# A smooth-quantised block of one decoder kernel: rounding in one pass, maxima and scaling read from PSUM, small operations merged over the batches, and the first product made turned

## The reference, cut to what matters

```python
def _smooth_quant_linear(x, w):
    amax_x = jnp.max(jnp.abs(x), axis=0)
    amax_w = jnp.max(jnp.abs(w), axis=0)
    s = jnp.sqrt(jnp.maximum(amax_x, EPS) / jnp.maximum(amax_w, EPS))
    s = jnp.maximum(s, EPS)
    xs = x / s
    ws = w * s
    x_scale = jnp.maximum(jnp.max(jnp.abs(xs), axis=-1, keepdims=True), EPS) / QMAX
    w_scale = jnp.maximum(jnp.max(jnp.abs(ws), axis=-1, keepdims=True), EPS) / QMAX
    x_q = jnp.clip(jnp.round(xs / x_scale), -QMAX, QMAX)
    w_q = jnp.clip(jnp.round(ws / w_scale), -QMAX, QMAX)
    return x_q @ w_q.T * x_scale * w_scale.T

def _expert_forward(xe, guw, dw):
    h = _smooth_quant_linear(xe, guw)
    gate, up = jnp.split(h, 2, axis=-1)
    a = jax.nn.silu(gate) * up
    return _smooth_quant_linear(a, dw)
```

## Time and profile before

| | us |
|---|---|
| median of three runs (2284.93 to 2288.26) | 2285.59 |
| the profiled execution | 2295.51 |
| its span, from first to last instruction | 2292.0 |
| the stage in it, from 587.01 (VectorE's first norm) to the end of the last addition on GpSimd | 81.6 |

### The profile page before, as it was taken

The page is one execution under the profiler, slowest core; times in us unless marked ns, Lnnn a source line. Parts: engine busy times, 40 slices in busy tenths (PEclk is TensorE's granted clock), DMA queues, the critical chain, the costliest instruction groups (busy, mean ns, idle before and its releaser), DMA issues.

```text
span 2292.0 us, 25579 instructions
## 1 busy us (share of the span) xinstructions
PE 1893.9 (83%) x9043; PEld 1207.4 (53%) x9048; DVE 1282.8 (56%) x2985; ACT 770.6 (34%) x1813; POOL 268.1 (12%) x254
## 2 busy tenths in 40 slices
PE   5685666888459599999856949899999899998698
PEld 3441223645345366666544636455555477777455
DVE  5738998654864444444487476433333666665222
ACT  4115454104122133333430612333332455554111
POOL 2611000000113200000020020000000222220111
PEclk9796877989758799999976979999999899999799
DMA  3010000000433300000000030300000200001300
GB/s 144 1 44 11 0 0 20 14 15 2 188 132 111 113 0 1 1 1 0 27 11 1 2 148 1 129 1 1 1 0 1 112 1 1 1 1 47 127 28 18
DMA packets 17373, 83.39 MB, mean 36 GB/s; under 512 B 3137, under 2 KB 9925, under 8 KB 13153
## 3 DMA queue, kind: packets, MB, share of 16 engines
q1 hardware_dynamic: 11168, 71.61, 7.9%
q0 software_dynamic: 2944, 8.03, 1.2%
q10 hardware_dynamic: 3136, 2.13, 0.3%
HBM read 73.49 MB, written 8.81 MB: 36 GB/s over the span
## 4 chain that ended last, share of the span: by engine, by line
PE 69%; DVE 18%; issue 6%; POOL 3%; ACT 2%; DMA 1%; another core or an unknown queue 0%; POOLq 0%; SPq 0%; DVEq 0%; ACTq 0%
PE bank L136 56%; PE bank L141 8%; PE bank L3330 3%; DVE space L795 2%; PE bank L3352 2%; DVE space L784 2%; DVE space L2881 1%; DVE space L1359 1%; DVE space L178 1%; DMA space<-in_L_attn 1%; POOL space L625 1%; POOL space L639 1%; ACT space L2936 0%; DVE space L1521 0%; DVE space L272 0%
## 5 line engine op out<-in xcount | busy, mean ns | idle before, releaser
L136 PE MATMUL bank<-space 128*128 128x256 f32 (+15 forms) x6725 | 1460.7, 426 | 102.3 <-DVE space L2881 18.5
L136 PEld LDWEIGHTS bank<-space 128*128 128x128 f32 (+7 forms) x6730 | 893.0, 183 | 621.0 <-issue 394.5
L141 PE MATMUL bank<-consts,space 128*128 128x128 f32 (+1 forms) x1610 | 259.9, 306 | 213.7 <-DVE space L189 67.0
L141 PEld LDWEIGHTS bank<-consts,space 128*128 128x128 f32 (+1 forms) x1610 | 205.8, 155 | 283.1 <-issue 157.3
L136 PE MATMUL bank<-space,consts 128*128 128x512 f32 (+2 forms) x148 | 90.8, 751 | 56.2 <-DVE space L790 49.1
L197 POOL TENSOR_TENSOR space<-space,consts 128x4 f32<-128x4 f32 x22 | 24.9, 1131 | 637.8 <-DVE space L184 637.8
L2571 POOL TENSOR_TENSOR space<-space,consts 128x4 f32<-128x4 f32 x64 | 68.6, 1072 | 220.7 <-DVE space L2502 220.7
L2320 DVE TENSOR_REDUCE space<-bank 128x2 f32<-128x512 f32 x64 | 44.0, 688 | 86.9 <-PE bank L136 86.8
L2366 ACT ACTIVATE space<-bank,space 128x256 f32<-128x256 f32 x128 | 59.5, 470 | 95.7 <-DVE space L2320 95.7
L136 PEld LDWEIGHTS bank<-space,consts 128*128 128x128 f32 x148 | 31.8, 237 | 99.2 <-DVE space L790 70.5
L2494 DVE TENSOR_REDUCE space<-bank 128x2 f32<-128x512 f32 x64 | 44.2, 691 | 71.1 <-PE bank L136 71.1
(11 more groups left out here) (344 smaller groups left out, 1983.2 us busy)
## 6 DMA issues: line engine op xcount, KB each, us to landing
space<-in_L_ffn SPq DMA_DIRECT2D x13, 2048.0 KB, 12.3
space<-in_L_attn SPq DMA_DIRECT2D x10, 2048.0 KB, 13.3
space<-in_L_xattn SPq DMA_DIRECT2D x4, 2048.0 KB, 9.7
expert_results<-space SPq DMA_DIRECT2D x16, 128.0 KB, 2.9
space<-expert_results SPq DMA_DIRECT2D x8, 256.0 KB, 4.7
space<-in_L_xattn SPq DMA_DIRECT2D x1, 1919.0 KB, 20.1
space<-in_L_xattn SPq DMA_DIRECT2D x1, 1536.0 KB, 6.2
space<-in_L_attn SPq DMA_DIRECT2D x1, 1074.5 KB, 4.9
```

What stands on the lines that cost most here:

```text
L136: return self.nc.tensor.matmul(out, lhsT, rhs, start=first, stop=last, skip_group_check=True)
L141: return self.nc.tensor.transpose(out, src, eye)
```

## The change

Both classes are rewritten; nothing else is touched. What is done after it:

- All small operations cover the four batches at once (`aw`, `ax`, `factor`, `inverse`, `scale`, `unit` are one tile each for all batches). The matrix maxima of `up` are taken first, those of `down` already during `up` (`weigh`).
- The maxima of the normed tokens are read from the PSUM banks into which they were turned, and ScalarE scales them from there into SBUF (`scale_tokens`); the copies of `Turned` are gone. VectorE scales `up`'s matrix; in `down` VectorE scales the tokens and ScalarE the matrix.
- TensorE turns the tokens (banks 4 to 7) and directly after them the matrix (banks 0 to 3), and VectorE takes the row maxima of both before anything is rounded.
- Rounding is one pass: times the reciprocal scale plus ROUND, left in f32. ScalarE does it for all tokens and for matrix batches 1 and 3 (Identity with a scale and a bias, both a column of SBUF), VectorE for matrix batches 0 and 2. The clips are gone. TensorE turns the f32 values (before: bf16), and the subtraction of ROUND is done by the copy from PSUM to bf16.
- The row of scales is a product of the scale column, broadcast to 128x128 as weights, with the identity, two of 128 columns per batch (before: one of 256 columns). The diagonal is gone.
- The first product is made turned (`tokens_out=False`): outputs on partitions, tokens along the row. Its tail is one multiplication with the row of token scales (`timed`), silu with the matrix scale, one `scalar_tensor_tensor` (`gated`) and the maximum for `down`; the eight turns and four copies between the linears are gone.
- At the end VectorE adds to x; GpSimd has only the norm's two operations left.

The removed lines are those of the functions above, marked "..." here.

```diff
 class SmoothLinear:
     N = 2
...
+    def __init__(self, c, w, kc, xs, rounded, tokens_out):
+        self.c, self.w, self.kc, self.xs, self.tokens_out = c, w, kc, xs, tokens_out
...
+        self.scale, self.unit = [c.sb(B, self.N) for _ in range(2)], [c.sb(B, self.N) for _ in range(2)]
+        self.t, self.row = rounded, c.bufs(B, S)
+        self.q = [[c.sb(kc, S, dt=BF16) for _ in range(B)] for _ in range(2)]
         self.s = c.signals(
...
     def tensor(self, e):
...
+        c, s, bk, n, kc, width = self.c, self.s, self.c.banks, self.N, self.kc, self.width
+        for b in range(B):
+            e.wait_ge(*s.x_scaled(b + 1))
+            self.back(bk[4 + b], self.xs(b)).then_inc(*s.x_back.one)
+        for b in range(B):
+            e.wait_ge(*s.w_scaled(b + 1))
+            self.back(bk[b], self.w(b)).then_inc(*s.w_back.one)
+        for b in range(B):
+            e.wait_ge(*s.x_rounded(b + 1))
+            self.again(bk[4 + b], self.t[0][b]).then_inc(*s.x_turned.one)
+        for b in range(B):
+            e.wait_ge(*(s.w_by_scalar if b % 2 else s.w_by_vector)(b // 2 + 1))
+            self.again(bk[b], self.t[1][b]).then_inc(*s.w_turned.one)
+        for b in range(B):
+            e.wait_ge(*(s.x_by_scalar if b % 2 else s.x_by_vector)(b // 2 + 1))
+            if self.tokens_out:
+                e.wait_ge(*(s.wq_by_scalar if b % 2 else s.wq_by_vector)(b // 2 + 1))
+            row = bk[b if self.tokens_out else 4 + b]
+            for i in range(n):
+                done = c.mm(row[:, i * P:(i + 1) * P],
+                            self.scale[1 if self.tokens_out else 0][:, b, i:i + 1].broadcast_to([P, P]), c.ident)
+            done.then_inc(*s.row_mm.one)
+            if not self.tokens_out:
+                e.wait_ge(*(s.wq_by_scalar if b % 2 else s.wq_by_vector)(b // 2 + 1))
+            left, right, out = (self.q[0][b], self.q[1][b], bk[4 + b]) if self.tokens_out else (self.q[1][b], self.q[0][b], bk[b])
+            for i in range(n):
                 for k in range(kc):
...
+                    done = c.mm(out[:, i * S:(i + 1) * S], left[:, k, i * P:(i + 1) * P], right[:, k, :], k == 0, k == kc - 1)
+            done.then_inc(*s.out_mm.one)
+    def back(self, bank, src):
+        for i in range(self.N):
+            for k in range(self.kc):
+                at = i * self.width + k * P
+                done = self.c.turn(bank[:, at:at + P], src[:, k, i * P:(i + 1) * P])
+        return done
+    def again(self, bank, src):
+        for k in range(self.kc):
+            for i in range(self.N):
+                at = k * S + i * P
+                done = self.c.turn(bank[:, at:at + P], src[:, i, k * P:(k + 1) * P])
+        return done
+    def weigh(self, e):
+        c, nc = self.c, self.c.nc
         for b in range(B):
...
+            nc.vector.tensor_reduce(self.aw[:, :, b], self.w(b), AX.X, ALU.max,
+                                    apply_absolute_value=True).then_inc(*c.v.next())
+        e.wait_ge(*c.v.so_far)
+        nc.vector.tensor_scalar(self.aw, self.aw, SQ_EPS, None, ALU.max).then_inc(*c.v.next())
+        e.wait_ge(*c.v.so_far)
+        nc.vector.reciprocal(self.aw, self.aw).then_inc(*c.v.next())
+    def factors(self, e):
+        c, s, nc = self.c, self.s, self.c.nc
+        e.wait_ge(*c.v.so_far)
+        nc.vector.scalar_tensor_tensor(out=self.ax, in0=self.ax, scalar=SQ_EPS, in1=self.aw, op0=ALU.max,
+                                       op1=ALU.mult).then_inc(*s.ratio.one)
+        e.wait_ge(*s.root.all)
+        nc.vector.tensor_scalar(self.factor, self.root, SQ_EPS, None, ALU.max).then_inc(*c.v.next())
+        e.wait_ge(*c.v.so_far)
+        nc.vector.reciprocal(self.inverse, self.factor).then_inc(*s.factors.one)
+    def units(self, e, j, ready, signal):
+        c, nc = self.c, self.c.nc
+        for b in range(B):
+            e.wait_ge(*ready(b + 1))
+            rows3 = c.banks[b if j else 4 + b][:, 0:self.N * self.width].rearrange("p (a b) -> p a b", b=self.width)
+            nc.vector.tensor_reduce(self.scale[j][:, b, :], rows3, AX.X, ALU.max,
+                                    apply_absolute_value=True).then_inc(*c.v.next())
+        e.wait_ge(*c.v.so_far)
+        nc.vector.tensor_scalar(self.scale[j], self.scale[j], SQ_EPS, 1.0 / QMAX, ALU.max, ALU.mult).then_inc(*c.v.next())
+        e.wait_ge(*c.v.so_far)
+        nc.vector.reciprocal(self.unit[j], self.scale[j]).then_inc(*signal.one)
+    def vector(self, e, scaled):
+        c, s, nc, n, width = self.c, self.s, self.c.nc, self.N, self.width
+        self.factors(e)
+        scaled(e)
+        self.units(e, 0, s.x_back, s.x_unit)
+        self.units(e, 1, s.w_back, s.w_unit)
+        e.wait_ge(*s.w_unit.all)
+        for b in range(0, B, 2):
+            for i in range(n):
+                done = nc.vector.tensor_scalar(self.t[1][b][:, i, :], c.banks[b][:, i * width:(i + 1) * width],
+                                               self.unit[1][:, b, i:i + 1], ROUND, ALU.mult, ALU.add)
+            done.then_inc(*s.w_by_vector.one)
+        for j, (ready, signal) in enumerate(((s.x_turned, s.x_by_vector), (s.w_turned, s.wq_by_vector))):
+            for b in range(0, B, 2):
+                e.wait_ge(*ready(b + 1))
+                nc.vector.tensor_scalar(flat(self.q[j][b]), c.banks[b if j else 4 + b][:, 0:self.kc * S], ROUND, None,
+                                        ALU.subtract).then_inc(*signal.one)
+    def scalar(self, e, bias, scaled):
+        c, s, nc, n, width = self.c, self.s, self.c.nc, self.N, self.width
+        e.wait_ge(*s.ratio.all)
+        nc.scalar.activation(self.root, self.ax, ACT.Sqrt).then_inc(*s.root.one)
+        e.wait_ge(*s.factors.all)
+        scaled(e)
+        e.wait_ge(*s.x_unit.all)
         for b in range(B):
             for i in range(n):
...
+                done = nc.scalar.activation(self.t[0][b][:, i, :], c.banks[4 + b][:, i * width:(i + 1) * width], ACT.Identity,
+                                            scale=self.unit[0][:, b, i:i + 1], bias=bias[:, 0:1])
+            done.then_inc(*s.x_rounded.one)
+        e.wait_ge(*s.w_unit.all)
+        for b in range(1, B, 2):
             for i in range(n):
...
+                done = nc.scalar.activation(self.t[1][b][:, i, :], c.banks[b][:, i * width:(i + 1) * width], ACT.Identity,
+                                            scale=self.unit[1][:, b, i:i + 1], bias=bias[:, 0:1])
+            done.then_inc(*s.w_by_scalar.one)
+        for j, (ready, signal) in enumerate(((s.x_turned, s.x_by_scalar), (s.w_turned, s.wq_by_scalar))):
             for b in range(1, B, 2):
...
+                e.wait_ge(*ready(b + 1))
+                nc.scalar.activation(flat(self.q[j][b]), c.banks[b if j else 4 + b][:, 0:self.kc * S], ACT.Identity,
+                                     bias=bias[:, 1:2]).then_inc(*signal.one)
         for b in range(B):
             e.wait_ge(*s.row_mm(b + 1))
...
+            nc.scalar.activation(self.row[b], c.banks[b if self.tokens_out else 4 + b][:, 0:S],
+                                 ACT.Copy).then_inc(*s.row_out.one)
 class SmoothQuant(Stage):
     def __init__(self, c, w, ld):
         self.c, self.w, self.ld = c, w, ld
...
+        self.up = SmoothLinear(c, lambda b: w["guT"][:, :, b, :], DC, lambda b: xs[:, :, b * S:(b + 1) * S],
+                               [[xn[:, 2 * b:2 * b + 2, :] for b in range(B)], c.bufs(B, 2, S)], False)
+        self.down = SmoothLinear(c, lambda b: w["downT"][:, b:b + 1, :], 1, lambda b: self.aT[b],
+                                 [c.bufs(B, 2, P), c.bufs(B, 2, P)], True)
...
     def tensor(self, e):
         c, s, bk = self.c, self.s, self.c.banks
...
+        for g in range(2):
+            e.wait_ge(*self.norm.s.normed(4 * g + 4))
+            for k in range(DC):
+                for i in range(4):
+                    done = c.turn(bk[2 * g + k][:, i * P:(i + 1) * P], self.xn[:, 4 * g + i, k * P:(k + 1) * P])
+                done.then_inc(*s.x_turned.one)
+        e.wait_ge(*self.up.s.x_scaled.all)
         self.up.tensor(e)
+        self.down.tensor(e)
+    def turned(self, b, k):
+        return self.c.banks[2 * (b // 2) + k][:, b % 2 * S:(b % 2 + 1) * S]
+    def vector(self, e):
+        c, w, s, bk, nc, up, down = self.c, self.w, self.s, self.c.banks, self.c.nc, self.up, self.down
+        nc.vector.memset(self.bias[:, 0:1], ROUND)
+        nc.vector.memset(self.bias[:, 1:2], -ROUND).then_inc(*s.bias.one)
+        self.norm.vector(e)
+        e.wait_ge(*self.ld.all)
+        up.weigh(e)
+        for g in range(2):
+            for k in range(DC):
+                e.wait_ge(*s.x_turned(2 * g + k + 1))
+                nc.vector.tensor_reduce(up.ax[:, k, 2 * g:2 * g + 2], bk[2 * g + k].rearrange("p (b s) -> p b s", s=S),
+                                        AX.X, ALU.max, apply_absolute_value=True).then_inc(*c.v.next())
+        def scale_weights(e):
+            e.wait_ge(*up.s.factors.all)
+            for b in range(B):
```

(58 more changed lines are left out.)

190 lines of the change are left out of this document (12 added, 178 removed).

## The result

The changed kernel takes 2261.51 us, the median of four runs (2254.09 to 2265.62), against 2286.93 for the kernel before in the same comparison: a ratio of 0.9885, with a 95% interval of 0.9857 to 0.9913. Run again later beside other runs of the kernel before it came to 2264.4 (five runs) and a ratio of 0.9888 (0.9869 to 0.9907). The difference of the first medians is 25.4 us, of the second 26.9.

A forecast was written before the change was run, and what follows sets the result against it. The prediction took the stage as a serial chain bound by VectorE; its links plus allowance ended it at 643.2 instead of 668.6, 25.4 earlier, so 2285.6 - 25.4 = 2260.2 us, range 2254.5 to 2268.5.

The forecast's parts named there:

- the allowance: Whole stage: 0.04 added for each of some 25 handovers between engines, putting the stage's end at 643.2.
- (a): Start of `up`: norm, matrix and token maxima, small operations and root; factors ready at 599.83, before 602.76.
- (b) to (d): `up`: ScalarE scales tokens (token scales 608.16), matrix scales follow at 611.0, ScalarE rounds to 614.4, last turn ends 615.0.
- (e): Row and main products of `up`: 0.48 + 0.48 per batch at full clock, ending at 619.0; before 634.1.
- the rival of half clock throughout: TensorE's clock falls again or does not rise in `up`: end 648.0, 20.6 saved, 2265.0; chance 0.15.
- (f): Between the linears: row copies, silu table load of 1.28 on the path, silus, `gated` and maxima; factors of `down` at 625.5.
- (g): Start of `down` at half clock: scaling, turns, maxima; token scales at 628.8, matrix scales at 630.5.
- (h): `down`: ScalarE's twelve roundings of 0.41 end at 633.8, the last turn at 634.3.
- (i): Tail of `down`: rows and products 0.86 + 0.43 per batch to 639.8; VectorE, 1.41 per batch, ends at 642.2.
- A load of 2.0 each: Slower case: 32 broadcast-column weight loads on the path; end 675, kernel 2292; slower or near nothing had chance 0.03.

The follow-up runs named there:

- a4: The changed kernel, but TensorE turns the tokens back before it turns the matrix; stage 63.93 us.
- a6: The changed kernel with turned tokens copied to SBUF, token maxima read there and VectorE scaling the tokens; stage 57.71 us.
- a2: The changed kernel with an unread root at the stage's start and an unread silu after `scale_tokens`, loading both tables early; stage 51.69 us.
- the 28 turns alone: The changed kernel with 28 unread identity turns on TensorE while it waits for the scaled tokens; stage 53.34 us.
- the combination: The changed kernel with both tables early, 28 unread turns, silus between row copies with later maxima, GpSimd adding batches 0 and 1; 2254.24 us, ratio 0.9842.

## Why the prediction was right

Forecast 2260.2, measured 2261.5; the stage 56.2 with the allowance (55.2 without), measured 54.4; VectorE 44.5, measured 45.3; ScalarE about 27, measured 27.4. The chain of links is what the runs bear out; that the totals agree to 1.3 us is in part luck, as the stage came 1.8 us shorter than forecast, a total moves by more than that from run to run, and the errors below cancelled in part.

- (a), the factors: 1.3 late. The step said "the root (0.21 and handover)" and put nothing for a table load there. It looked where the silu's load would stand and not where the root's would, once the copies ahead of it were gone.
- (b) to (d): right in mechanism, with ScalarE over-priced by 0.06 per operation. Over scaling and rounding that gave back 0.9, so that token scales came 0.9 late and the last token rounding 0.5 late.
- (e): the clock rose in 604 to 606, ahead of most matrix turns, and held through the thin stretch of roundings; the rival of half clock throughout did not come about. The variants a4 and a6 show that it was a near thing: there it fell again before the products (0.50 in 610 to 612, and 0.61 on average in 614 to 618). What the full clock was worth no run measured by itself. The prediction's time for the rise, 607.7, follows from no row that it shows; that the rise came just as long after the start of the stage (20.7: the mean of 0.78 in 604 to 605 puts it near 604.4) is luck.
- (f): the silu's table stood on the chain as said (a2).
- (g), (h): right to 0.3. (i): the clock rose in 631 to 632 instead of staying low, and batches followed at 0.67 after the first instead of 1.29. So the products of `down` were not the slowest part of the tail, as the prediction had listed among its signs; VectorE's 1.38 per batch was, for which it had 1.41. That is why so much faster products brought the end only 0.8 earlier.
- The allowance of 1.0 for handovers was not needed.
- The Trainium skill adds a drain to every switch of tables in "ScalarE: Activation LUTs", What ACT_TABLE_LOAD costs. The trace shows none: the silu began at 616.98, 0.01 after its load of 1.28 from 615.69, and the load 0.02 after the last row copy.
- The Trainium skill says in "TensorE: Matmul & The Clock Gate", Part 4: PE-mode transpose, that full rate does not engage for transposes. The trace disagrees: from 600.93 on TensorE did nothing but turns, and the granted clock rose in 604 to 606.
- Both operands' maxima before any rounding I treated as one link of several. Two parts stand out: this order with 9.6, and the one-pass rounding with 10.8 (9.4 and the table load that came on the chain in its variant). Reading and scaling from PSUM gave 3.4 to 4.4, merging 3.0. These were measured singly, two in the kernel before and two in the changed one, where the order's 9.6 includes turns at half clock. They need not add up: the sum is 26.8 to 27.8 for a stage that saved 27.3, so nothing can be read from it for the turned product, which no run tried alone. The link that it shortens, from the last product of `up` to the factors of `down`, went from 8.1 to some 6.7, with the silu's load now on it.
- One sign of being wrong did come: other stages moved by more than 2 us, the fourth by 2.4. It said nothing of the change, as these lengths move as much between two profiles of one kernel (129.6 and 134.8 for the fourth).
- Three sums in the prediction do not come out. The range of 2254.5 to 2268.5 is not what its cases with 1.5 on each side give (2256.2 to 2269.9). A load of 2.0 each, by its own 0.21 hidden, would end the stage near 700 and not at 675. And half clock at (e) is 624.2 in one place and 4.8 more than 619.0, so 623.8, in another. None of them enters the forecast.

## What to carry to other kernels

Where engines take turns, write the chain down link by link with start-to-start prices; a sum of such rows held here to 1 us in 55, though it had the first link 1.3 too short and the one from the matrix scales to the last product of `up` 0.9 too long, and the two partly cancelled. Ask of every operand what the next engine could begin on before the first has finished its phase. When work leaves an engine, look at what had been hiding behind it: a table load that followed an early copy can come to stand on the chain, and one unread operation in an idle stretch takes it off again (1.0 and 1.6 us here). An experiment on one part can bring such a load in too, so compare its trace link by link before its total is read.

## What the runs showed that I had not expected

A table load is not always early: in the changed kernel the root's load began at 595.88, after the ratio was ready, while the one before `down` began 0.02 after the last silu, 0.9 ahead of need. That ScalarE had done nothing in the stage before it is not the whole reason, as the variant with one-pass rounding alone shows, where two copies stood before it. What the two late loads have in common is two waits directly ahead of the root, for the start of the stage or for the bias and then for the ratio; the early loads shown here had one or none. No run tried the number of waits by itself. Stages that no kernel touched moved by several us, the fourth from 129.6 to 134.8. And keeping TensorE busy ahead of time gave a full clock in one kernel and not in another: with the 28 turns alone it fell just after 605, 4.7 us after the unread turns had ended and as the useful ones had just begun; in the combination the useful ones came a us sooner and it was worth 1.2.
